# Conv chunks behind blocks 0, 1, 2, 3, and another order of three engines' queues in the last step of layer 0, in a two-layer feed-forward kernel

## The chip, the cores and the metric

One core of one Trainium2 chip (trn2). The metric is the device time of one execution in microseconds (us). The kernel before took 2215.2 us (median of 3 runs, 2212.43 to 2218.39).

## The reference

What is computed, on x of shape (128, 64, 1024), read as 8192 rows of 1024:

```
x = x + L0_ffn(L0_cond(x))     # L0_cond: per batch a 64x64 mixing matrix, made from 8 by a small network with softmax
x = x + L1_ffn(L1_cond(x))     # L1_cond: conv over 9 taps along the 1024, 4 groups of 16 channels, plus a bias per batch
# L0_ffn: x W_base^T + b, plus 8 experts of rank 16, weighed by softmax(gates) minus a threshold, clipped at 0, normalized
# L1_ffn: x W_base^T + b, plus 8 experts of rank 16, weighed by the softmax of the two largest gates
```

## The kernel before, in words

**Tiles and steps.** A tile is 128 rows (two batches) by 1024. There are 64 tiles in layer 0 and 64 in layer 1 and so 128 steps n = 0 to 127; STEPS is 64. `run` (L183) calls each engine's `step(j, par, lay0, lay, lay1, lay2)` with n = 2j + par and the layers of tiles n-1, n, n+1 and n+2; the first two and the last two steps of each layer are written out, the others are a hardware loop. Layer 0 stores its result twice, as rows and as blocks that layer 1 reads. Every product of two fp32 values is made from a high part (fp32r) and a low one (the difference): Xhi/Xlo, Yhi/Ylo, Whi/Wlo, HThi/HTlo.

**A step on TensorE (L911).** For each of KT = 8 blocks k it runs `base` (L847: 9 matmuls of tile n, Yhi and Ylo by Whi and Wlo, into psB), and between blocks it puts three other things: `turn` (L869) of tile n-1, a transpose of the weighed low-rank product hw; `up` (L877) of tile n-1, six matmuls by Bhi/Blo that read HThi and HTlo; and `mix` (L817) of tile n+1 in four chunks c = 0 to 3, in layer 0 the mixing matrix, in layer 1 the conv (six matmuls each, L842 to L844). In the loop over k the order is base, turn, chunks, up. Where they stand is set by hand (L54 to L57):

```
MIX_AFTER = (0, 1, 2, 3)
CONV_AFTER = (0, 0, 1, 1)
TURN_AFTER, UP_AFTER = (4, 2), (5, 3)
```

that is, in layer 1 `turn` stands after k=2 and `up` after k=3. CONV_AFTER holds for chunks of a tile of layer 1, so from step 63 on. Chunks use two halves of psT in turn, so in layer 1 chunk c waits for the side copy of chunk c-2 (side_out, L830). Block 0 waits for half 0 of Yhi and Ylo and for `emit` of tile n-2 (o_done, L854), block 4 for half 1; in step 64 each block also waits for its new weights (w_hi, w_lo, w_loP, L855).

**The other engines in a step of layer 1.** Each works its queue in program order.

- VectorE (L757): `weigh` of tile n-1 (copy ag and the gates, L742 to L734, then hw, L748); `evacuate_y` of tile n+1 (L604) chunk by chunk out of psT; `low_ht` (HTlo, L755), `add_rest` (L633), `add_shifted` of half 0 (L612), `emit` of tile n-1 (three additions, L648), `split_y` of half 0 (Ylo, L618), then half 1 of both.
- ScalarE (L497): its part of the gates, `copy_side` (L460) of the four chunks, the part of the conv's result that belongs to a neighbour; `high_ht` (HThi, L552), `high_x` of tile n+2 (Xhi, L431), `split_y` (Yhi, L447) of each half once `add_shifted` has run.
- GpSimd (L390): `low_x` of tile n+2 (Xlo, L356), `residual` of tile n+1 (L385).
- SyncE (L255): loads Xraw and row of tile n+2, sends the side parts to their neighbours (`shift`, L303, four transfers, after all four copies), stores tile n-1, loads res of tile n+1.

**The last step of layer 0 (n = 63).** Here the weights of layer 1 replace those of layer 0, block by block as `base` is done with them: ScalarE writes Whi (`split_w`, L462, which waits for base_tile > k), VectorE Wlo of even k (L622) and GpSimd Wlo of odd k (`split_lo`, L344). VectorE's order is evacuate_y 0 and 1, split_w 0, evacuate_y 2 and 3, split_w 2, add_shifted and split_y of half 0, low_ht, add_rest, half 1, split_w 4, emit; split_w 6 comes at step 64. ScalarE has copy_side 0 and 1, split_w 0, copy_side 2 and 3, split_w 1 to 3, Yhi of half 0, high_ht, Yhi of half 1, split_w 4 and 5, high_x, split_w 6 and 7. GpSimd has split_lo 1, 3, 5, low_x, split_lo 7, residual.

Of the kernel before, what the change touches and what calls it, by code (L numbers as in the profile page):

```python
# [30 lines left out]
KT = H // P  # L31
# [6 lines left out]
BR = 8  # L38
# [13 lines left out]
STORE0 = 16 * (1 + BG)  # L52
MODES = 8
MIX_AFTER = (0, 1, 2, 3)  # L54
CONV_AFTER = (0, 0, 1, 1)
MIX_AFTER_FIRST = (1, 3, 4, 5)
TURN_AFTER, UP_AFTER = (4, 2), (5, 3)  # L57
PIECES = 4
# [12 lines left out]
def build(nc, x, condw, condr, mixw, l0w, l0b, l0B, convw, l1w, l1b, l1B, out):  # L71
# [8 lines left out]
    with ExitStack() as ctx:  # L80
# [121 lines left out]
        def before(j, par):  # L202

            return (j, 0) if par else (j - 1, 1)

        def after(j, par):

            return (j + 1, 0) if par else (j, 1)
# [123 lines left out]
        def _(pool):  # L332
# [11 lines left out]
            def split_lo(k, layer):  # L344
                pool.wait_ge(w_hi, KT * layer + k + 1)
                w = H + NAG[layer]
                pool.tensor_tensor(Wlo[:, k, 0:w], stage[:, k, 0:w], as_f32(Whi[:, k, 0:w]), ALU.subtract)\
                    .then_inc(w_loP, 1)
# [41 lines left out]
            def step(j, par, lay0, lay, lay1, lay2):  # L390
                n = 2 * j + par
                if isinstance(j, int) and n == 0:

                    pool.wait_ge(w_hi, KT)
                    pool.wait_ge(w_lo, KT // 2)
                    pool.wait_ge(w_loP, KT // 2)
                    pool.memset(craw, 0.0).then_inc(conv_zero, 1)
                if isinstance(j, int) and n == STEPS - 1:
                    for k in range(1, KT - 2, 2):
                        split_lo(k, 1)  # L400
                if lay2 is not None:
                    low_x(j + 1, par, lay2)
                if isinstance(j, int) and n == STEPS - 1:
                    split_lo(KT - 1, 1)
                if lay1 is not None:
                    residual(*after(j, par), lay1)
                if isinstance(j, int) and n == 1:
                    pool.wait_ge(s_hi, 2)
                    pool.tensor_tensor(Blo[:, 1, :], b1raw, as_f32(Bhi[:, 1, :]), ALU.subtract).then_inc(s_loP, 1)
                    pool.wait_ge(s_hi, 3)  # L410
                    pool.tensor_tensor(CT[:, :, 1, :, :], craw, as_f32(CT[:, :, 0, :, :]), ALU.subtract)\
                        .then_inc(s_loP, 1)
# [5 lines left out]
        def _(act):  # L418
# [14 lines left out]
            def high_m(n):  # L433
                act.wait_ge(agg_ready, n + 1)
                nc.scalar.copy(M[0:C, 0, 0:C], agg[0:C, :])
                nc.scalar.copy(M[C:P, 0, C:P], agg[C:P, :]).then_inc(m_hi, 1)
# [10 lines left out]
                    nc.scalar.copy(Yhi[:, par, h * HB:(h + 1) * HB], Y[:, h * HB:(h + 1) * HB])\  # L447
                        .then_inc(yhi_half, 1)

            def copy_side(j, par, c):  # L450

                m = 2 * j + par - STEPS
                act.wait_ge(y_chunk, NC * (m + STEPS) + c + 1)
                if isinstance(m, int) and m == 0:
                    act.wait_ge(agg_ready, STEPS)
                else:
                    act.wait_ge(y_sum, 2 * m)
                bank = psT[:, c % 2, :].rearrange("p (b s t o) -> p b s t o", b=2, s=2, t=BR)
                to = side.rearrange("p h (t b o) -> p b (h t) o", t=REACH, b=BG)
                nc.scalar.copy(to[:, 2 * c:2 * c + 2], bank[:, :, 1]).then_inc(side_out, 1)  # L460

            def split_w(k, layer):  # L462
                act.wait_ge(w_in[k], 16 * (layer + 1))
                if layer:

                    if k < KT - 1:
                        act.wait_ge(base_tile, k + 1)
                    else:
                        act.wait_ge(base_done, STEPS)
                w = H + NAG[layer]  # L470
                nc.scalar.copy(Whi[:, k, 0:w], stage[:, k, 0:w]).then_inc(w_hi, 1)
# [25 lines left out]
            def step(j, par, lay0, lay, lay1, lay2):  # L497
                n = 2 * j + par
                last_of_0 = isinstance(j, int) and n == STEPS - 1
                if lay0 is not None:  # L500
                    weigh(*before(j, par), lay0)
                if lay1 == 1:
                    for c in range(NC):
                        copy_side(*after(j, par), c)
                        if last_of_0 and c == 1:
                            split_w(0, 1)
                if last_of_0:
                    for k in range(1, KT // 2):
                        split_w(k, 1)
                if lay1 == 1 and not last_of_0:  # L510
                    high_ht(*before(j, par))
                    if lay2 is not None:
                        high_x(j + 1, par, lay2)
                if lay1 is not None:
                    split_y(*after(j, par), lay1, range(0, 1))
                if lay1 == 0 and lay2 is not None:
                    high_x(j + 1, par, lay2)
                if (lay1 != 1 or last_of_0) and lay0 is not None:
                    high_ht(*before(j, par))
                if lay1 is not None:  # L520
                    split_y(*after(j, par), lay1, range(1, 2))
                if lay2 == 0:
                    high_m(n + 2)
                if last_of_0:
                    for k in range(KT // 2, KT - 2):
                        split_w(k, 1)
                    high_x(j + 1, par, lay2)
                if isinstance(j, int) and n == 1:
                    act.wait_ge(l1s_in, 16)
                    nc.scalar.copy(Bhi[:, 1, :], b1raw).then_inc(s_hi, 1)  # L530
                    act.wait_ge(conv_in, 16 * 2 * BR)
                    nc.scalar.copy(CT[:, :, 0, :, :], craw).then_inc(s_hi, 1)
                if isinstance(j, int) and n == STEPS - 1:
                    for k in range(KT - 2, KT):
                        split_w(k, 1)

            def weigh(j, par, layer):

# [21 lines left out]
        def _(dve):  # L560
# [196 lines left out]
            def step(j, par, lay0, lay, lay1, lay2):  # L757
                n = 2 * j + par
                last_of_0 = isinstance(j, int) and n == STEPS - 1
                if lay0 is not None:  # L760
                    weigh(*before(j, par), lay0)
                if isinstance(j, int) and n == STEPS:
                    split_w(KT - 2, 1)
                if lay1 == 0:
                    evacuate_y(*after(j, par), 0, range(0, 2))
                    if lay2 == 0:
                        mixing_matrix(n + 2)
                    evacuate_y(*after(j, par), 0, range(2, 3))
                    split_y(*after(j, par), 0, range(0, 1))
                    evacuate_y(*after(j, par), 0, range(3, NC))  # L770
                    if lay0 is not None:
                        low_ht(*before(j, par))
                        add_rest(*before(j, par))
                    split_y(*after(j, par), 0, range(1, 2))
                    if lay2 == 0:
                        low_m(n + 2)
                    if lay0 is not None:
                        emit(*before(j, par), lay0)
                elif last_of_0:
                    evacuate_y(*after(j, par), 1, range(0, 2))  # L780
                    split_w(0, 1)
                    evacuate_y(*after(j, par), 1, range(2, NC))
                    split_w(2, 1)
                    add_shifted(*after(j, par), 0)
                    split_y(*after(j, par), 1, range(0, 1))
                    low_ht(*before(j, par))
                    add_rest(*before(j, par))
                    add_shifted(*after(j, par), 1)
                    split_y(*after(j, par), 1, range(1, 2))
                    split_w(4, 1)  # L790
                    emit(*before(j, par), lay0)
                elif lay1 == 1:
                    evacuate_y(*after(j, par), 1, range(NC))
                    low_ht(*before(j, par))
                    add_rest(*before(j, par))
                    add_shifted(*after(j, par), 0)
                    emit(*before(j, par), lay0)
                    split_y(*after(j, par), 1, range(0, 1))
                    add_shifted(*after(j, par), 1)
                    split_y(*after(j, par), 1, range(1, 2))  # L800
                else:
                    low_ht(*before(j, par))
                    add_rest(*before(j, par))
                    emit(*before(j, par), lay0)
# [172 lines left out]
```

## Time and profile before

| what | value |
|---|---|
| median of 3 runs | 2215.2 us (2212.43 to 2218.39) |
| profiled execution | 2212.12 us, span 2209.8 us |
| mean granted TensorE clock | 0.996 |
| TensorE busy | 2152.9 us (97%), 12684 matmuls |
| VectorE, ScalarE, GpSimd busy | 65%, 23%, 39% |
| chain that ended last | TensorE 92%, VectorE 4%, issue 1%, DMA 1%, ScalarE 1%, GpSimd 1% |

The span runs from the first to the last instruction of the profiled execution. L862 is line 862 of the kernel; `out<-in` names what an instruction writes and reads. A number in square brackets behind a row of a timeline is the time for which that engine stood idle before it, and what ended that. Of matmuls the ends are modelled: several overlap, so their busy times add up to more than the spacing of their starts.

### The profile page before, as it was taken

The numbers are of one execution on the slowest core, as the hardware profiler recorded it, in microseconds if no ns is written. First come the engines' busy times: TensorE is split into PE (matmuls) and PEld (weight loads), VectorE is DVE, ScalarE is ACT, GpSimd is POOL, SyncE is SP. The second block draws the span as 40 slices with busy tenths as digits, with TensorE's granted clock in tenths as the row PEclk, the third lists the DMA queues.
The fourth block names the chain that finished last, engine by engine and source line by source line (L and its number), as shares of the span: only waits on it lengthen the run. The fifth ranks groups of instructions, "written<-read, shape, count | busy, mean of one in ns | idle before, by whom it ended". The sixth has DMA issues, their size and how long they took to land.

```text
span 2209.8 us, 41168 instructions
## 1 busy us (share of the span) xinstructions
PE 2152.9 (97%) x12684; PEld 2097.4 (95%) x12684; DVE 1446.7 (65%) x3539; ACT 503.2 (23%) x1179; POOL 862.6 (39%) x1052
## 2 busy tenths in 40 slices
PE   4999999999999999999899999999999999999998
PEld 4999999999999999999799999999999999999997
DVE  6777777777777777777555655656556665556665
ACT  3212221221222122221322222222222222222221
POOL 5534444343444434344533333333333333333331
PEclk9999999999999999999999999999999999999999
DMA  5433433334343333434444333343333343333432
GB/s 169 129 108 89 112 96 106 102 99 109 89 109 98 105 103 99 109 89 110 149 135 138 119 118 126 117 134 131 117 122 122 128 136 118 120 124 125 132 124 76
DMA packets 163554, 256.34 MB, mean 116 GB/s; under 512 B 21072, under 2 KB 103376, under 8 KB 163536
## 3 DMA queue, kind: packets, MB, share of 16 engines
q1 hardware_dynamic: 163232, 255.55, 37.7%
q10 hardware_dynamic: 304, 0.56, 0.1%
q8 instruction: 9, 0.15, 0.0%
q14 instruction: 9, 0.07, 0.0%
HBM read 122.01 MB, written 100.73 MB: 101 GB/s over the span
## 4 chain that ended last, share of the span: by engine, by line
PE 92%; DVE 4%; issue 1%; DMA 1%; ACT 1%; POOL 1%; DVEq 0%; SPq 0%; ACTq 0%
PE psB L862 71%; PE psB L888 8%; PE psT L838 3%; PE psT L842 3%; PE psT L843 2%; PE psT L844 2%; PE psT L839 1%; PE psB L875 1%; DVE small L729 1%; DVE small L734 0%; DVE small L731 0%; DVE Y L604 0%; DMA shifted<-mixbuf 0%; DMA stage<-in_l0w 0%; ACT mixbuf L460 0%
## 5 line engine op out<-in xcount | busy, mean ns | idle before, releaser
L862 PE MATMUL psB<-Whi,Yhi 128*128 128x384 f32 (+2 forms) x3072 | 736.7, 348 | 5.5 <-issue 5.5
L356 POOL TENSOR_TENSOR Xlo<-Xraw,Xhi 128x256 fp32r<-128x256 f32 x512 | 423.9, 860 | 786.1 <-ACT Xhi L431 786.0
L862 PE MATMUL psB<-Wlo,Yhi 128*128 128x384 f32 (+2 forms) x3072 | 714.1, 340 | 0.0
L862 PE MATMUL psB<-Whi,Ylo 128*128 128x384 f32 (+2 forms) x3072 | 711.7, 340 | 0.0
L862 PEld LDWEIGHTS psB<-Whi,Ylo 128*128 128x128 f32 x3072 | 560.3, 189 | 0.0
L862 PEld LDWEIGHTS psB<-Wlo,Yhi 128*128 128x128 f32 x3072 | 559.7, 189 | 0.0
L862 PEld LDWEIGHTS psB<-Whi,Yhi 128*128 128x128 f32 x3072 | 526.3, 190 | 22.3 <-issue 5.7
L385 POOL TENSOR_TENSOR res<-res,bias 128x256 f32<-128x256 f32 x256 | 183.8, 749 | 394.2 <-DMA res<-x_scratch 394.2
L447 ACT CAST Yhi<-Y 128x512 fp32r<-128x512 f32 x256 | 159.2, 622 | 562.0 <-DVE Y L612 302.6
L375 POOL TENSOR_TENSOR res<-Xraw,bias 128x256 f32<-128x256 f32 x256 | 223.1, 906 | 114.8 <-DVE outb L648 114.8
L648 DVE TENSOR_TENSOR outb<-psB,res 128x384 f32<-128x384 f32 (+1 forms) x384 | 227.8, 683 | 29.1 <-PE psB L888 21.4
L618 DVE TENSOR_TENSOR Ylo<-Y,Yhi 128x512 fp32r<-128x512 f32 x256 | 212.1, 829 | 49.2 <-ACT Yhi L447 49.2
L742 DVE COPY ag<-psB 128x138 f32<-128x138 f32 (+1 forms) x128 | 38.5, 301 | 209.9 <-PE psB L862 209.9
L431 ACT CAST Xhi<-Xraw 128x1024 fp32r<-128x1024 f32 x128 | 134.7, 1052 | 167.2 <-PE psT L839 154.7
L604 DVE TENSOR_TENSOR Y<-psT,row 128x256 f32<-128x256 f32 x256 | 101.9, 417 | 101.0 <-PE psT L844 100.8
L460 ACT COPY mixbuf<-psT 128x256 f32<-128x256 f32 x256 | 89.4, 374 | 316.7 <-DVE Y L604 316.7
L842 PE MATMUL psT<-CT,Xhi 128*128 128x256 f32 x512 | 149.9, 293 | 7.9 <-ACT mixbuf L460 7.2
L838 PE MATMUL psT<-M,Xhi 128*128 128x256 f32 x512 | 132.9, 312 | 22.3 <-DVE M L575 13.2
L755 DVE TENSOR_TENSOR HTlo<-psB,HThi 128x128 fp32r<-128x128 f32 x128 | 37.3, 292 | 174.4 <-ACT HThi L552 174.4
L612 DVE TENSOR_TENSOR Y<-shifted,Y 128x512 f32<-128x512 f32 x128 | 102.8, 803 | 71.7 <-DMA shifted<-mixbuf 71.7
L844 PE MATMUL psT<-CT,Xlo 128*128 128x256 f32 x512 | 145.2, 284 | 0.0
L843 PE MATMUL psT<-CT,Xhi 128*128 128x256 f32 x512 | 145.2, 284 | 0.0
(90 smaller groups left out, 2056.5 us busy)
## 6 DMA issues: line engine op xcount, KB each, us to landing
Xraw<-in_x SPq DMA_DIRECT2D x64, 512.0 KB, 3.4
x_scratch<-outb SPq DMA_DIRECT2D x64, 512.0 KB, 2.7
x_block_scratch<-outb SPq DMA_DIRECT2D x512, 64.0 KB, 2.0
Xraw<-x_block_scratch SPq DMA_DIRECT2D x64, 512.0 KB, 4.9
res<-x_scratch SPq DMA_DIRECT2D x64, 512.0 KB, 4.4
out<-outb SPq DMA_DIRECT2D x64, 512.0 KB, 3.0
shifted<-mixbuf SPq DMA_DIRECT2D x128, 224.0 KB, 2.5
row<-row_scratch SPq DMA_DIRECT2D x128, 64.0 KB, 4.3
```

The source lines that it names most:

```text
L356: last = pool.tensor_tensor(Xlo[:, piece], Xraw[:, par, piece], as_f32(Xhi[:, piece]), ALU.subtract)
L375: last = pool.tensor_tensor(res[:, par, :].rearrange("p (r q) -> p r q", r=BR)[:, r, :], Xraw[:, par, 0:H].rearrange("p (q r) -> p r q", r ...
L385: last = pool.tensor_tensor(res[:, par, piece], res[:, par, piece], bias[:, piece], ALU.add)
L447: nc.scalar.copy(Yhi[:, par, h * HB:(h + 1) * HB], Y[:, h * HB:(h + 1) * HB])\
L618: nc.vector.tensor_tensor(Ylo[:, par, h * HB:(h + 1) * HB], Y[:, h * HB:(h + 1) * HB], as_f32(Yhi[:, par, h * HB:(h + 1) * HB]), ALU.subtr ...
L648: last = nc.vector.tensor_tensor(to[:, r0:r1, :], product, res[:, par, :].rearrange("p (r q) -> p r q", r=BR)[:, r0:r1, :], ALU.add)
L838: mm(to, Xhi[:, xs], M[:, :, :].rearrange("p s n -> p (s n)"), start=True, stop=False)
L842: mm(to, Xhi[:, xs], hi, start=True, stop=False)
L843: mm(to, Xhi[:, xs], lo, start=False, stop=False)
L844: last = mm(to, Xlo[:, xs], hi, start=False, stop=True)
L862: last = mm(psB[:, 3 * par + b, 0:cols], y, w[:, k, BANK0[b]:BANK0[b] + cols], start=(k == 0 and y is yh and w is Whi), stop=(k == KT - 1 ...
L888: last = mm(psB[:, 3 * par + b, :], y[:, :], w[:, layer, b * HB:(b + 1) * HB], start=False, stop=(y is HTlo), skip_group_check=True)
```

## The change

CONV_AFTER becomes (0, 1, 2, 3). In the last step of layer 0 the order of the queues is another: VectorE takes evacuate_y of all chunks, split_w 0 and 2, low_ht, add_rest, half 0 of Y, emit, half 1; its split_w 4 and 6 move to step 64, behind chunks 1 and 3. ScalarE interleaves split_w with the rest and has high_ht and high_x ahead of the halves of Y. GpSimd has split_lo 1 and 3, low_x, split_lo 5 and 7. `copy_side` takes a range of chunks and waits for y_sum or agg_ready at chunk 0 only. The other steps keep their order.

```diff
-CONV_AFTER = (0, 0, 1, 1)
+CONV_AFTER = (0, 1, 2, 3)
...
                 if isinstance(j, int) and n == STEPS - 1:
-                    for k in range(1, KT - 2, 2):
+                    for k in range(1, KT // 2, 2):
                         split_lo(k, 1)
                 if lay2 is not None:
                     low_x(j + 1, par, lay2)
                 if isinstance(j, int) and n == STEPS - 1:
-                    split_lo(KT - 1, 1)
+                    for k in range(KT // 2 + 1, KT, 2):
+                        split_lo(k, 1)
...
-            def copy_side(j, par, c):
+            def copy_side(j, par, chunks):
...
+                for c in chunks:
+                    act.wait_ge(y_chunk, NC * (m + STEPS) + c + 1)
+                    if c == 0:
+                        if isinstance(m, int) and m == 0:
+                            act.wait_ge(agg_ready, STEPS)
+                        else:
+                            act.wait_ge(y_sum, 2 * m)
...
+                elif last_of_0:
+                    split_w(0, 1)
+                    split_w(1, 1)
+                    copy_side(*after(j, par), range(0, 2))
+                    split_w(2, 1)
+                    copy_side(*after(j, par), range(2, NC))
+                    split_w(3, 1)
+                    high_ht(*before(j, par))
+                    high_x(j + 1, par, lay2)
+                    split_w(4, 1)
+                    split_y(*after(j, par), 1, range(0, 1))
+                    split_w(5, 1)
+                    split_w(6, 1)
+                    split_y(*after(j, par), 1, range(1, 2))
+                    split_w(7, 1)
+                elif lay1 == 1:
+                    copy_side(*after(j, par), range(NC))
                     high_ht(*before(j, par))
                     if lay2 is not None:
                         high_x(j + 1, par, lay2)
...
+                    split_y(*after(j, par), 1, range(2))
...
-                if isinstance(j, int) and n == STEPS:
-                    split_w(KT - 2, 1)
...
                 elif last_of_0:
-                    evacuate_y(*after(j, par), 1, range(0, 2))
+                    evacuate_y(*after(j, par), 1, range(NC))
                     split_w(0, 1)
-                    evacuate_y(*after(j, par), 1, range(2, NC))
                     split_w(2, 1)
+                    low_ht(*before(j, par))
+                    add_rest(*before(j, par))
                     add_shifted(*after(j, par), 0)
                     split_y(*after(j, par), 1, range(0, 1))
-                    low_ht(*before(j, par))
-                    add_rest(*before(j, par))
+                    emit(*before(j, par), lay0)
                     add_shifted(*after(j, par), 1)
                     split_y(*after(j, par), 1, range(1, 2))
-                    split_w(4, 1)
-                    emit(*before(j, par), lay0)
                 elif lay1 == 1:
-                    evacuate_y(*after(j, par), 1, range(NC))
+                    evacuate_y(*after(j, par), 1, range(0, 2))
+                    if isinstance(j, int) and n == STEPS:
+                        split_w(4, 1)
+                    evacuate_y(*after(j, par), 1, range(2, NC))
+                    if isinstance(j, int) and n == STEPS:
+                        split_w(6, 1)
                     low_ht(*before(j, par))
                     add_rest(*before(j, par))
                     add_shifted(*after(j, par), 0)
```

## Rows read from the trace of the kernel before

**Rows 1.** TensorE's waits over the whole span: engine line <- what it waited for: us in total, times, longest.

```profile
...
PE psB L888 <- DVE HTlo L755: 7.7, 2, 6.9
PE psT L842 <- ACT mixbuf L460: 7.2, 16, 2.6
...
```

**Rows 2.** The transposes (line 875) of layer 1: count, ns min/median/max, first and last start.

```profile
...
L875 PE MATMUL psB<-ident,hw x63: 270/270/270, 1099.9 to 2175.6; 128*128 128x128 f32 x63
...
```

**Rows 3.** TensorE's timeline, two transposes of layer 1: start, us, engine, line, operation.

```profile
...
1465.02 0.27 PE L875 MATMUL psB<-ident,hw 128*128 128x128 f32 x1
...
1482.16 0.27 PE L875 MATMUL psB<-ident,hw 128*128 128x128 f32 x1
...
```

**Rows 4.** TensorE's timeline, first matmuls of steps 63, 64 and 65.

```profile
...
1060.48 0.70 PE L862 MATMUL psB<-Whi,Yhi 128*128 128x384 f32 x3
...
1087.07 0.34 PE L862 MATMUL psB<-Whi,Yhi 128*128 128x384 f32 x1
...
1109.36 0.34 PE L862 MATMUL psB<-Whi,Yhi 128*128 128x384 f32 x1
...
```

**Rows 5.** TensorE's timeline, one step of layer 1: blocks 0 and 2, first chunk, `up`.

```profile
...
1612.65 0.70 PE L862 MATMUL psB<-Whi,Yhi 128*128 128x384 f32 x3
...
1614.25 0.28 PE L842 MATMUL psT<-CT,Xhi 128*128 128x256 f32 x1
...
1618.79 0.70 PE L862 MATMUL psB<-Whi,Yhi 128*128 128x384 f32 x3
...
1622.10 0.40 PE L888 MATMUL psB<-Bhi,HThi 128*128 128x512 f32 x1
...
```

**Rows 6.** The same step on VectorE and ScalarE, in brackets the idle time before and its cause.

```profile
...
1616.30 0.74 DVE L604 TENSOR_TENSOR Y<-psT,row 128x256 f32<-128x256 f32 x2
...
1616.82 0.65 ACT L460 COPY mixbuf<-psT 128x256 f32<-128x256 f32 x2 [3.15 <-DVE Y L604]
...
1618.99 0.42 DVE L604 TENSOR_TENSOR Y<-psT,row 128x256 f32<-128x256 f32 x1 [0.29 <-PE psT L844]
...
1619.45 0.37 ACT L460 COPY mixbuf<-psT 128x256 f32<-128x256 f32 x1 [0.35 <-DVE Y L604]
...
1620.68 0.27 ACT L552 CAST HThi<-psB 128x128 fp32r<-128x128 f32 x1 [0.86 <-PE psB L875]
...
1620.98 0.29 DVE L755 TENSOR_TENSOR HTlo<-psB,HThi 128x128 fp32r<-128x128 f32 x1 [1.57 <-ACT HThi L552]
...
1622.68 0.69 DVE L612 TENSOR_TENSOR Y<-shifted,Y 128x512 f32<-128x512 f32 x1 [1.07 <-DMA shifted<-mixbuf]
...
1627.84 0.69 DVE L618 TENSOR_TENSOR Ylo<-Y,Yhi 128x512 fp32r<-128x512 f32 x1 [0.69 <-ACT Yhi L447]
...
```

**Rows 7.** The timeline at the kernel's end: HTlo, then the last `up`.

```profile
...
2202.57 0.29 DVE L755 TENSOR_TENSOR HTlo<-psB,HThi 128x128 fp32r<-128x128 f32 x1 [0.72 <-ACT HThi L552]
...
2203.01 0.70 PE L888 MATMUL psB<-Bhi,HThi 128*128 128x512 f32 x2 [0.77 <-DVE HTlo L755]
...
2203.55 0.63 PE L888 MATMUL psB<-Blo,HThi 128*128 128x512 f32 x2
...
```

**Rows 8.** VectorE's weight subtractions (line 625): ns min/median/max, first and last start.

```profile
...
L625 DVE TENSOR_TENSOR Wlo<-stage,Whi x8: 1357/1370/3089, 21.3 to 1093.1; 128x1162 fp32r<-128x1162 f32 x4, 128x1160 fp32r<-128x1160 f32 x4
...
```

**Rows 9.** VectorE's timeline in the last step of layer 0: shifted part added, tile 62 emitted.

```profile
...
1077.63 0.69 DVE L612 TENSOR_TENSOR Y<-shifted,Y 128x512 f32<-128x512 f32 x1 [4.25 <-DMA shifted<-mixbuf]
...
1083.92 1.34 DVE L648 TENSOR_TENSOR outb<-psB,res 128x384 f32<-128x384 f32 x3
...
```

**Rows 10.** TensorE after two waits (timeline), then both stretches with clock (PEclk), by engine.

```profile
...
80.82 0.38 PE L838 MATMUL psT<-M,Xhi 128*128 128x256 f32 x1 [2.21 <-DVE Y L599]
...
1095.26 0.45 PE L842 MATMUL psT<-CT,Xhi 128*128 128x256 f32 x1 [2.56 <-ACT mixbuf L460]
...
81.00:85.00 4.00, 4.00 (x18) 4.00 (x19) 3.54 (x7) 0.62 (x1) 0.00 (x0) 0.58 1.02 414
1095.26:1098.83 3.57, 3.57 (x15) 3.57 (x16) 0.85 (x2) 0.92 (x3) 1.86 (x3) 0.52 0.00 0
...
```

More of the change, by code:

```diff
@@ L448, in split_y @@
                         .then_inc(yhi_half, 1)
-            def copy_side(j, par, c):
+            def copy_side(j, par, chunks):
                 m = 2 * j + par - STEPS
[L453 to L460, printed above, removed]
+                for c in chunks:
[5 more added lines that the diff above has]
+                            act.wait_ge(y_sum, 2 * m)
+                    bank = psT[:, c % 2, :].rearrange("p (b s t o) -> p b s t o", b=2, s=2, t=BR)
+                    to = side.rearrange("p h (t b o) -> p b (h t) o", t=REACH, b=BG)
+                    nc.scalar.copy(to[:, 2 * c:2 * c + 2], bank[:, :, 1]).then_inc(side_out, 1)
             def split_w(k, layer):
@@ L501, in step @@
                     weigh(*before(j, par), lay0)
[L502 to L510, printed above, removed]
+                if lay1 == 0:
+                    split_y(*after(j, par), 0, range(0, 1))
+                    if lay2 is not None:
+                        high_x(j + 1, par, lay2)
+                    if lay0 is not None:
+                        high_ht(*before(j, par))
+                    split_y(*after(j, par), 0, range(1, 2))
+                    if lay2 == 0:
+                        high_m(n + 2)
+                elif last_of_0:
[5 more added lines that the diff above has]
+                    split_w(3, 1)
+                    high_ht(*before(j, par))
+                    high_x(j + 1, par, lay2)
+                    split_w(4, 1)
[6 more added lines that the diff above has]
+                    copy_side(*after(j, par), range(NC))
                     high_ht(*before(j, par))
@@ L513, in step @@
                         high_x(j + 1, par, lay2)
[L514 to L518, printed above, removed]
-                    high_ht(*before(j, par))
[L520 to L527, printed above, removed]
+                    split_y(*after(j, par), 1, range(2))
+                else:
+                    high_ht(*before(j, par))
                 if isinstance(j, int) and n == 1:
@@ L532, in step @@
                     nc.scalar.copy(CT[:, :, 0, :, :], craw).then_inc(s_hi, 1)
-                if isinstance(j, int) and n == STEPS - 1:
-                    for k in range(KT - 2, KT):
-                        split_w(k, 1)
             def weigh(j, par, layer):
```

## The prediction

> **What bounds the kernel now.** I read the page first: TensorE's busy share stands in the table of the profile above and leaves 3% of the span, so the other engines matter only where TensorE waits for them. The table of who waited for whom comes next [rows 1]: layer 1 holds 7.2 us of waits of conv matmuls (L842) for ScalarE's copies of a chunk's side parts, and one wait of 6.9 us in the last step of layer 0, where `up` (L888) needs HTlo. That table leaves out the tails of matmuls, so I measured the steps themselves by TensorE's transposes (`turn`, L875), one in a step. Between the first and the last of layer 1's 63 of them lie 1075.7 us [rows 2], 62 steps, 17.35 us each; a step in which nothing is waited for takes 17.14 [rows 3]. So all that layer 1's steps can gain is 1075.7 - 62 x 17.14 = 13.0 us, and around the change of layers there is a second, larger loss: steps 63 and 64 start at 1060.48 and 1087.07 and step 65 at 1109.36 [rows 4], 48.88 us for what takes 34.28 undisturbed, a loss of 14.6. Nothing else that the change touches can give time back: 27.6 us, 1.2%, is its ceiling.
>
> **Where a step of layer 1 has its slack.** In the timeline of one step [rows 5] a base block takes 1.60 us (1612.65 to 1614.25), chunks 0 and 1 follow at 0.72 each (the 6.14 us to 1618.79 less two blocks, over four, less a few hundredths of waiting), then block 1, chunks 2 and 3, block 2, the transpose, block 3 and `up` at 1622.10. The last chunk ends at 1618.79; `up` comes 3.31 us later. In that gap VectorE takes chunk 3 out of PSUM (1618.99), ScalarE copies its side part (1619.45), makes HThi (1620.68), and VectorE makes HTlo (1620.98) [rows 6]. The programs fix this order: ScalarE has high_ht behind all four copy_side, VectorE has low_ht behind all four evacuate_y. It costs nothing today, because two base blocks and a transpose lie between chunk 3 and `up`.
>
> **Part 1, CONV_AFTER (0, 1, 2, 3), the term that decides.** Chunk 3 moves behind block k=3. UP_AFTER[1] stays 3, and in a pass over k TensorE issues the chunk before `up`. So `up`, which waits for ht_hi and ht_lo, now follows chunk 3 with nothing between. What must pass in that hole, counted from the moment when TensorE could have started `up`: to evacuate_y of chunk 3, 0.20 us (1618.79 to 1618.99); to its side copy, 0.46 (to 1619.45); to HThi, right behind the copy on ScalarE, 0.28 (a copy is busy 0.37, and the second of two copies back to back starts 0.28 after the first: the pair takes 0.65 [rows 6]); to HTlo, 0.30 (1620.68 to 1620.98); from HTlo to `up`, 0.44, from the end of the kernel, where nothing else lies between (2202.57 to 2203.01). Sum 1.68. Restarting costs 0.07 more: there the first pair of `up`'s matmuls is busy 0.70, the next 0.63 [rows 7]. So **1.75 us a step**. Bounds: 1.5, if the last matmul's tail covers 0.2 of it; 2.1, if HTlo (busy 0.29) is stretched as VectorE's weight subtraction was beside GpSimd, from 1.37 to 3.09 [rows 8], which adds 0.36. It happens wherever conv and `up` of k=3 share a step, steps 64 to 126: 63 x 1.75 = **+110.3 us**. Nothing hides it: TensorE's queue is in order and is what sets the end.
>
> What the same edit takes away: chunk 2 may start once chunk 0's side copy is done. The gates (L742 to L748) hold VectorE until 3.65 us into the step (1616.30), so that copy ends at about 3.65 + 0.46 + 0.37 = 4.5, and chunk 2 is due at 2 x 1.60 + 2 x 0.72 = 4.6: any delay of the gates shows. The new place is 3 x 1.60 + 2 x 0.72 = 6.2 in, late enough even with the gates 0.7 behind. All 13.0 us go: **-13.0**.
>
> What else moves with chunk 3, by 3.3 us: SyncE's four shift transfers, and behind them in its queue the store, the res load and the next Xraw load. Chunk 3 leaves PSUM at about 9.5 into the step; the first add_shifted starts 3.23 after the side copy (1619.45 to 1622.68), that is at 13.2; then emit and both Ylo, as long as now (5.85, from 1622.68 to 1628.53), to 19.0. The step is then 18.9 long, so VectorE is just done when base_done comes, and the gates have 1.6 us to spare before the transpose and chunk 2. Ylo of half 0 is ready two microseconds early, o_done too. Xhi starts at 10.5 and Xlo ends near 15, before 20.5 where it is due; the Xraw load, issued near 17.6, has over 10 us. I take 0 for all of this; it costs something only if that tail grows by over 1.6 us.
>
> ScalarE's copy_side in one call saves three waits already met: 0.
>
> **Part 2, the last step of layer 0.** Today TensorE sits 6.9 us at `up` because ScalarE and VectorE keep HThi and HTlo behind half 0 of Y, which waits for a shift transfer until 1077.63 [rows 9]. Now they come first, and that wait falls to 0.4 to 2 us (two weight splits of 1.37 stand ahead of HTlo [rows 8]). What is late next: emit of tile 62 now stands behind the first Ylo, and block 0 of step 64 waits for o_done of that tile. The transfer is still late, since the weight, Xraw and bias loads ahead of it don't change. From 1077.63: 2.1 us to the end of the first Ylo (add 0.7, cast 0.6, subtract 0.7, handovers), 1.34 for emit [rows 9], so step 64 starts at about 1081.3, against 1087.07: -5.8. In step 64 the weighing starts late, behind half 1 of Y and ScalarE's last split, which I put at 1.7, and split_w(6) stands ahead of HTlo, 1.37; 17.14 + 1.7 + 1.37 = 20.2 against 22.29: -2.1 (its share of the 63 stalls is counted above). GpSimd's splits of k=5 and 7 move behind Xlo of tile 65; they are due ten microseconds later in step 64, 0. Together **-8**, between 0 (a new wait replaces each one removed) and -14.6.
>
> **Sum.** 110.3 - 13.0 - 8 = +89.3 us. The profiled execution took 2212.1 us (span 2209.8, and 2.3 around it that the change doesn't touch), so 2301.4; the median shown, 2215.2, is 3.1 above it: **2304.5**. By the bounds of the stall, 63 x 1.5 and 63 x 2.1, and of part 2: 2215.2 + 94.5 - 13 - 14.6 = 2282, and 2215.2 + 132.3 - 13 = 2334.
>
> **Rivals.**
> A, the clock. TensorE's granted clock fell after a wait of 2.56 us: 0.52 over the next 3.57 us, about the lower of its two levels (1.2 against 2.4 GHz), a loss of 3.57 x 0.48 = 1.7 us; it also fell after one of 2.21 (0.58 in the four microseconds from 81) [rows 10]. If the new wait did this in each step, 63 x 1.7 = 107 more: 2412. For it: the wait comes every step. Against: the profile will show it as about 1.5 us (the matmul's tail taken off), shorter than any wait after which the clock fell here, and today's waits of up to 0.4 leave it alone. Chance 0.05.
> The Trainium skill, "TensorE: Matmul & The Clock Gate", section "A second HAM failure mode: psum-queue depth-cycling", says that frequent short idles between groups of matmuls can make the clock swing between half and full rate. By that rule rival A would be the outcome; this trace, which idles briefly in many steps of layer 1 and has a mean clock of 0.996 all the same, doesn't bear it out for the shortest ones.
> B, VectorE becomes the second bound. If GpSimd's Xlo now overlaps emit and add_shifted worse than today, or the shift transfers land 3 us later, the tail passes the 1.6 us of slack and the gates hold chunk 2 and the transpose. 1 us beyond it costs 63: 2368. Against: the order of these operations and their spacing are the same as now. Chance 0.04.
> C, faster. The edit does what it is for, and `up` isn't held: the change is then -13 - 8 = -21, or 2194. The place is the handover from chunk 3 to HTlo; it decides at 21 / 63 = 0.33 us, below which the kernel gains. The chain as read is 1.68, and HTlo can't overtake chunk 3 on VectorE. Chance 0.03, with 0.01 for a result within 0.3%, which is about what a measurement of this kernel can tell from no change.
> Forecast: 0.88. Hence slower 0.96, same 0.01, faster 0.03, and a range of 2282 to 2334, which the forecast's own bounds fill.
>
> **What would show it.** Right: in the table of waits, TensorE L888 waiting for HTlo some 63 times, 1.5 us each, about 95 us in total; L842's wait for ScalarE's copy gone from layer 1; transposes 18.9 us apart, first to last in layer 1 about 1172; layer 0's steps at their old length; no 6.9 us wait, but a wait of L862 near 1080 for emit (L648). Wrong: transposes still 17.1 to 17.4 apart (rival C), a granted clock well under 1.0 in the middle of layer 1 (A), or TensorE waiting in `turn` or at chunk 2 (B).

## The result

The changed kernel takes 2299.5 us (median of 5 runs, 2297.2 to 2301.4) against 2215.2 for the kernel before (by now of 5 as well, 2211.5 to 2218.4): 1.038 times as long (95% interval 1.037 to 1.040). That is 84.3 us slower by the medians and 87.9 by the two profiled spans, which the page of the profile after shows with the busy shares and the chain that ended last:

```profile
span 2297.7 us, 40976 instructions
...
PE 2160.0 (94%) x12684; PEld 2104.6 (92%) x12684; DVE 1374.6 (60%) x3539; ACT 502.2 (22%) x1179; POOL 855.0 (37%) x1052
...
PE 92%; DVE 3%; issue 1%; ACT 1%; DMA 1%; POOL 0%; ACTq 0%; SPq 0%; DVEq 0%
```

TensorE does the same 12684 matmuls and is busy for 94% where it was 97%. Who it waited for (total us, times, longest), and its transposes in layer 1 (count, ns min/median/max, first and last start):

```profile
PE psB L895 <- DVE HTlo L761: 96.3, 64, 2.1
...
PE psB L869 <- issue: 7.9, 2, 5.2
...
PE psT L849 <- ACT mixbuf L463: 0.2, 1, 0.2
```

```profile
L882 PE MATMUL psB<-ident,hw x63: 270/270/270, 1086.7 to 2259.0; 128*128 128x128 f32 x63
```

The first row answers to [rows 1]: `up` (now L895) waits for HTlo 64 times, 96.3 us, where it was 7.7 in two; the conv's wait for the side copy has gone from 7.2 us to 0.2. From the first to the last transpose it is 1172.3 us, 1075.7 in [rows 2]. The hole in one step, the counterpart of [rows 5] and [rows 6]:

```profile
1619.98 0.28 PE L849 MATMUL psT<-CT,Xhi 128*128 128x256 f32 x1
...
1620.57 0.28 PE L851 MATMUL psT<-CT,Xlo 128*128 128x256 f32 x1
1620.89 0.42 DVE L610 TENSOR_TENSOR Y<-psT,row 128x256 f32<-128x256 f32 x1 [1.89 <-PE psT L851]
1621.35 0.37 ACT L463 COPY mixbuf<-psT 128x256 f32<-128x256 f32 x1 [1.95 <-DVE Y L610]
1621.61 0.27 ACT L558 CAST HThi<-psB 128x128 fp32r<-128x128 f32 x1
...
1621.92 0.29 DVE L761 TENSOR_TENSOR HTlo<-psB,HThi 128x128 fp32r<-128x128 f32 x1 [0.61 <-ACT HThi L558]
...
1622.36 0.70 PE L895 MATMUL psB<-Bhi,HThi 128*128 128x512 f32 x2 [1.51 <-DVE HTlo L761]
...
1622.90 0.63 PE L895 MATMUL psB<-Blo,HThi 128*128 128x512 f32 x2
...
1624.56 1.02 DVE L618 TENSOR_TENSOR Y<-shifted,Y 128x512 f32<-128x512 f32 x1 [2.02 <-DMA shifted<-mixbuf]
```

The last six matmuls are chunk 3's, 0.12 apart, so `up` could have started at 1620.69. Behind them come the evacuation (1620.89), the side copy (1621.35), HThi (1621.61), HTlo (1621.92) and `up` (1622.36): 0.20, 0.46, 0.26, 0.31 and 0.44, in all 1.67. In brackets stands 1.51, since the profile takes off the last matmul's tail.

Then the change of layers (before: [rows 4], [rows 9]):

```profile
1074.86 0.74 DVE L618 TENSOR_TENSOR Y<-shifted,Y 128x512 f32<-128x512 f32 x1 [3.22 <-DMA shifted<-mixbuf]
...
1076.34 1.09 DVE L624 TENSOR_TENSOR Ylo<-Y,Yhi 128x512 fp32r<-128x512 f32 x1 [0.74 <-ACT Yhi L448]
1077.36 1.34 DVE L654 TENSOR_TENSOR outb<-psB,res 128x384 f32<-128x384 f32 x3
...
1078.91 0.41 PE L869 MATMUL psB<-Whi,Yhi 128*128 128x384 f32 x1 [2.63 <-issue]
...
1090.83 1.37 DVE L631 TENSOR_TENSOR Wlo<-stage,Whi 128x1160 fp32r<-128x1160 f32 x1
...
1092.12 0.28 DVE L761 TENSOR_TENSOR HTlo<-psB,HThi 128x128 fp32r<-128x128 f32 x1
...
1092.55 0.70 PE L895 MATMUL psB<-Bhi,HThi 128*128 128x512 f32 x2 [2.09 <-DVE HTlo L761]
```

Step 63 starts at 1058.68 and step 64 at 1078.91, 20.23 us where it was 26.59: the first Ylo, emit (1077.36 to 1078.70), then block 0. Its row says `issue`, no releaser that the profile found; that it was emit is read from the 0.21 us between them, and from the run below that moves emit. Step 65 starts at 1101.94, 23.03 later, where it was 22.29: split_w(6) (it stood in step 64 before too, right behind the gates, and now stands behind chunk 3) starts at 1090.83 and pushes HTlo to 1092.12, and `up` waits 2.09 us instead of 1.51. The granted clock (PEclk, the first number behind the five engines) fell after both long waits and stayed up through layer 1:

```profile
1078.90:1083.00 4.10, 4.09 (x17) 4.10 (x18) 2.77 (x5) 2.24 (x5) 1.76 (x2) 0.61 0.66 193
1092.50:1096.50 4.00, 3.96 (x13) 3.55 (x14) 2.54 (x6) 0.62 (x1) 3.26 (x4) 0.62 0.42 130
1117.00:2259.00 1142.00, 1051.61 (x6242) 1022.41 (x6241) 560.73 (x1520) 244.38 (x544) 368.62 (x484) 1.00 0.35 114
```

**Where the 87.9 us of span come from**: steps 65 to 126 start to start (1101.94 to 2271.66, before 1109.36 to 2185.12), +94.0; steps 63 and 64, -5.6; layer 0 up to step 63 -1.8 and the last step with the end +1.4. The latter two are not the change's: in the ten runs below, whose layer 0 is the same up to there, step 63 starts anywhere between 1058.0 and 1060.0, a spread as wide as this difference, and at the end the clock fell around the same 2.33 us wait that it survived before.

### The profile page after: what moved, and what is told of

It is laid out like the page before. It is cut to its first block, busy times and chain, and to the rows that moved or that the text cites. A ratio compares the mean times of both kernels' runs of the same rounds, so it can differ in the third digit from the quotient of the medians.

```text
span 2297.7 us, 40976 instructions
## 1 busy us (share of the span) xinstructions
PE 2160.0 (94%) x12684; PEld 2104.6 (92%) x12684; DVE 1374.6 (60%) x3539; ACT 502.2 (22%) x1179; POOL 855.0 (37%) x1052
## 4 chain that ended last, share of the span: by engine, by line
PE 92%; DVE 3%; issue 1%; ACT 1%; DMA 1%; POOL 0%; ACTq 0%; SPq 0%; DVEq 0%
PE psB L869 70%; PE psB L895 8%; PE psT L845 3%; PE psT L851 3%; PE psT L849 3%; PE psT L850 3%; PE psT L846 1%; DVE Y L610 1%; DVE HTlo L761 1%; ACT HThi L558 1%; PE psB L882 1%; DMA stage<-in_l0w 0%; POOL Wlo L347 0%; DMA shifted<-mixbuf 0%; DMA outb<-in_condw 0%
## 5 line engine op out<-in xcount | busy, mean ns | idle before, releaser
L610 DVE TENSOR_TENSOR Y<-psT,row 128x256 f32<-128x256 f32 x256 | 108.6, 425 | 366.7 <-PE psT L851 364.2
L463 ACT COPY mixbuf<-psT 128x256 f32<-128x256 f32 x256 | 95.1, 372 | 498.3 <-DVE Y L610 498.3
L895 PE MATMUL psB<-Bhi,HThi 128*128 128x512 f32 x256 | 85.6, 416 | 96.3 <-DVE HTlo L761 96.3
L895 PEld LDWEIGHTS psB<-Bhi,HThi 128*128 128x128 f32 x256 | 42.8, 189 | 108.0 <-ACT HThi L558 105.4
```

The costliest lines, as they stand in the source:

```text
L895: last = mm(psB[:, 3 * par + b, :], y[:, :], w[:, layer, b * HB:(b + 1) * HB], start=False, stop=(y is HTlo), skip_group_check=True)
```

## The experiments

Theory 1 is the prediction's: the handover from chunk 3 through ScalarE and VectorE to `up`, 1.75 us in each of 63 steps. Ratios are to the kernel before on the same chip (2208 to 2210 us in those runs); the changed kernel itself was not run again beside them, so where 2299.5 is set against them, it is across chips. "Step" below is the mean distance of the transposes of steps 65 to 126: 17.35 before, 18.87 after.

**The two halves of the change, apart.** The first:

```diff
-CONV_AFTER = (0, 0, 1, 1)
+CONV_AFTER = (0, 1, 2, 3)
```

> Before, with CONV_AFTER (0, 1, 2, 3) alone; the last step of layer 0 keeps its queues. Theory 1 (the handover from chunk 3 to HTlo stands in front of up in each of 63 steps, 1.75 us each; the queue order has no part in it): 2215 + 110 - 13 for the old waits at chunk 2 - 3 to 4 for the 2.56 us wait in step 64 = about 2308, with 63 waits of up for HTlo of 1.5 us and the 6.9 us wait still there. Rival (the new queue order of ScalarE and VectorE holds TensorE, and up's wait only shows it): within 20 us of 2215.

Measured: 2303.8 us, ratio 1.043 (1.041 to 1.045), step 18.87; 95.4 us above the kernel before on that chip (2208.4), where 93 was expected. TensorE's waits of `up`:

```profile
PE psB L888 <- DVE HTlo L755: 103.1, 65, 7.4
```

This is the whole loss, with the old queue order: 63 waits of 1.5 (steps 64 to 126), the long wait of step 63, 7.4, and the last `up`'s, 0.8. The second half, the change with that line put back:

```diff
-CONV_AFTER = (0, 1, 2, 3)
+CONV_AFTER = (0, 0, 1, 1)
```

> After, with CONV_AFTER back at (0, 0, 1, 1). Theory 1: no wait at up in layer 1; the queue order alone gives 4 to 10 us at the change of layers, so about 2207, with the small waits at chunk 2 (13 us in sum) back. Rival (queue order is the cost): near 2299.

Measured: 2203.5 us, ratio 0.9975 (0.9966 to 0.9985), step 17.30. The waits at chunk 2 are back (1.6 us in step 63, where chunk 0's side copy now stands behind two weight splits, and 3.4 in step 64, where the gates are late), `up`'s wait is left at the end alone:

```profile
PE psT L849 <- ACT mixbuf L463: 8.4, 12, 3.4
...
PE psB L895 <- DVE HTlo L761: 0.8, 1, 0.8
```

So the queue order is a small gain, 5 us, and has no part in the loss.

**Undoing the handover alone.** Chunks stay behind k = 0, 1, 2, 3:

```diff
-                    copy_side(*after(j, par), range(NC))
+                    copy_side(*after(j, par), range(0, 3))
                     high_ht(*before(j, par))
+                    copy_side(*after(j, par), range(3, NC))
...
-                    evacuate_y(*after(j, par), 1, range(2, NC))
+                    evacuate_y(*after(j, par), 1, range(2, 3))
+                    low_ht(*before(j, par))
+                    evacuate_y(*after(j, par), 1, range(3, NC))
                     if isinstance(j, int) and n == STEPS:
                         split_w(6, 1)
-                    low_ht(*before(j, par))
```

> After, but in the steps of layer 1 high_ht stands ahead of the fourth copy_side on ScalarE and low_ht ahead of the fourth evacuate_y on VectorE; chunks stay behind k=0, 1, 2, 3. Theory 1: HTlo is ready about a microsecond before up is due, the 63 waits vanish, 2299.5 - 63 x 1.75 = 2189, layer 1's transposes 17.14 apart. Rival 2 (it is the four separate places of the chunks, or the shift transfers, emit and Y coming 3.3 us later, that hold TensorE): over 2250, with the wait moved to block 0, o_done or chunk 2.

Measured: 2188.3 us, ratio 0.9908 (0.9892 to 0.9925); repeated, 2188.5 and 0.9905 (below). Step 17.13, from 17.12 to 17.14 in all 61. Its timeline:

```profile
1602.98 0.37 ACT L463 COPY mixbuf<-psT 128x256 f32<-128x256 f32 x1 [2.04 <-DVE Y L611]
...
1603.25 0.27 ACT L559 CAST HThi<-psB 128x128 fp32r<-128x128 f32 x1
...
1603.55 0.29 DVE L762 TENSOR_TENSOR HTlo<-psB,HThi 128x128 fp32r<-128x128 f32 x1 [0.61 <-ACT HThi L559]
...
1604.64 0.63 PE L897 MATMUL psB<-Bhi,HThi 128*128 128x512 f32 x2
...
1605.30 0.38 ACT L463 COPY mixbuf<-psT 128x256 f32<-128x256 f32 x1 [1.78 <-DVE Y L611]
```

HTlo (1603.55) now stands ahead of chunk 3's copy (1605.30), and `up` starts at 1604.64 without a wait. Everything else that came later with chunk 3 is still late (the shift transfers, emit, Y), so none of it held TensorE: rival 2 of that run falls.

**Is the hole a sum of its links?** ScalarE's half of that edit alone:

```diff
-                    copy_side(*after(j, par), range(NC))
+                    copy_side(*after(j, par), range(0, 3))
                     high_ht(*before(j, par))
+                    copy_side(*after(j, par), range(3, NC))
```

> After, with ScalarE's half of the former alone: high_ht ahead of the fourth copy_side, VectorE's order as it is. Theory 1, the chain is a sum of links: copy and HThi (0.46 + 0.28 + 0.30) leave it, VectorE's own 0.33 from chunk 3 to HTlo takes their place, so 0.20 + 0.33 + 0.44 + 0.07 = 1.04 us a step instead of 1.75: 2299.5 - 63 x 0.71 = 2255, waits of up of about 0.8 us each. Rival 3 (only the last handover to up counts, or the wait comes from VectorE alone): no gain, 2299, or the whole of it, 2189.

Measured: 2256.0 us, ratio 1.0215 (1.0198 to 1.0232), step 18.16, that is 1.03 above the step without a wait; 1.04 was expected.

```profile
1601.13 0.27 ACT L559 CAST HThi<-psB 128x128 fp32r<-128x128 f32 x1
...
1602.72 0.42 DVE L611 TENSOR_TENSOR Y<-psT,row 128x256 f32<-128x256 f32 x1 [1.89 <-PE psT L852]
1603.06 0.28 DVE L762 TENSOR_TENSOR HTlo<-psB,HThi 128x128 fp32r<-128x128 f32 x1
1603.18 0.37 ACT L463 COPY mixbuf<-psT 128x256 f32<-128x256 f32 x1 [1.78 <-DVE Y L611]
...
1603.49 0.70 PE L896 MATMUL psB<-Bhi,HThi 128*128 128x512 f32 x2 [0.81 <-DVE HTlo L762]
```

HThi (1601.13) is done long before; VectorE goes from chunk 3 (1602.72) to HTlo (1603.06) in 0.34, and `up` follows 0.43 later. One link more, in the other direction, was ScalarE's Xhi ahead of HThi:

```diff
                     copy_side(*after(j, par), range(NC))
-                    high_ht(*before(j, par))
                     if lay2 is not None:
                         high_x(j + 1, par, lay2)
+                    high_ht(*before(j, par))
```

> After, with ScalarE's high_x (1.06 us) ahead of high_ht in layer 1: the chain gets a link of about 0.97 us, the wait of up grows from 1.51 to about 2.5 us a step. Theory 1, every link counts at its full length: 62 x 0.97 = 60 more, 2360, if the clock stays. Rival A of the prediction, the clock falls after waits of this size: each fall about 1.7 us more, so up to 2465 if it falls in every step, and the granted clock of layer 1 well below 1.0. The trace has one fall after a wait of 2.1 and one after 2.6 and none after the 1.5 of 62 steps; I expect falls in a part of the steps, 2380 to 2440.

Measured: 2398.5 us, ratio 1.086 (1.085 to 1.088). `up` waits 2.45 us in each step, and the clock falls in every second one:

```profile
1499.76 0.27 PE L882 MATMUL psB<-ident,hw 128*128 128x128 f32 x1
...
1505.51 0.70 PE L895 MATMUL psB<-Bhi,HThi 128*128 128x512 f32 x2 [2.45 <-DVE HTlo L761]
1506.05 0.63 PE L895 MATMUL psB<-Blo,HThi 128*128 128x512 f32 x2
...
1519.56 0.27 PE L882 MATMUL psB<-ident,hw 128*128 128x128 f32 x1
...
1525.33 1.20 PE L895 MATMUL psB<-Bhi,HThi 128*128 128x512 f32 x2 [2.45 <-DVE HTlo L761]
1526.32 1.05 PE L895 MATMUL psB<-Blo,HThi 128*128 128x512 f32 x2
...
1540.72 0.27 PE L882 MATMUL psB<-ident,hw 128*128 128x128 f32 x1
```

From transpose to transpose it is 19.80 us, then 21.16, and so on to the end, 31 long and 30 short of 61. In a short one the pairs of `up` are 0.54 and 0.47 apart, in a long one 0.99 and 0.85. The granted clock behind the two waits (first number behind the five engines):

```profile
1505.51:1509.51 4.00, 4.00 (x21) 3.73 (x22) 2.92 (x5) 0.62 (x1) 2.71 (x4) 1.00 0.33 108
1525.33:1529.33 4.00, 4.00 (x13) 3.42 (x14) 1.93 (x4) 0.62 (x1) 2.67 (x4) 0.63 0.34 107
```

The short step is 0.94 above 18.86, the link that was put in; the long one pays 1.36 more for the clock. 61 x 0.94 + 31 x 1.36 = 99.5, and 2398.5 - 99.5 = 2299.0, within a microsecond of the changed kernel's time.

**Covering the handover instead of shortening it.** Two ways of putting one block of 1.60 us between chunk 3 and `up`:

```diff
-TURN_AFTER, UP_AFTER = (4, 2), (5, 3)
+TURN_AFTER, UP_AFTER = (4, 2), (5, 4)
```

> After, with up of layer 1 behind block k=4 instead of k=3: the queues as they are, only the consumer moves. Theory 1: the handover of 1.68 us from the end of chunk 3 now has a block of 1.60 to hide under, so about 0.1 us a step stays: 2299.5 - 63 x 1.65 = 2196, a little above the run with HThi and HTlo ahead of chunk 3. Rival 2 (late emit and Y become the bound once up moves another 1.6 us back): VectorE's tail passes the end of the step, TensorE waits at block 0 or for the gates, 2215 or more.

Measured: 2201.0 us, ratio 0.9958 (0.9942 to 0.9975), step 17.31. And, in a kernel of its own:

```diff
-CONV_AFTER = (0, 1, 2, 3)
+CONV_AFTER = (0, 1, 2, 2)
```

> After, with CONV_AFTER (0, 1, 2, 2): chunk 3 follows chunk 2 at once and up keeps its place behind k=3. Theory 1: again one block of 1.60 us covers a chain of 1.68, about 0.1 us a step stays, 2299.5 - 63 x 1.65 = 2196; chunk 2's small waits don't come back, since chunk 2 keeps its place. Rival (any conv chunk moved late costs in proportion): half of the loss, near 2250.

Measured: 2198.5 us, ratio 0.9949 (0.9932 to 0.9965), step 17.26. Both give the loss back but for 0.18 and 0.13 us a step over 17.13: the cover is 0.08 short of the chain, and the restart is paid. In one step with `up` behind k=4:

```profile
1628.54 0.69 PE L869 MATMUL psB<-Whi,Yhi 128*128 128x384 f32 x3
...
1629.78 0.29 DVE L761 TENSOR_TENSOR HTlo<-psB,HThi 128x128 fp32r<-128x128 f32 x1 [0.61 <-ACT HThi L558]
...
1630.21 0.70 PE L895 MATMUL psB<-Bhi,HThi 128*128 128x512 f32 x2
...
1631.68 0.70 PE L869 MATMUL psB<-Whi,Yhi 128*128 128x384 f32 x3
```

`up` follows HTlo by 0.43, the link of the chain. The block ahead of it takes 1.67 us and `up` 1.47, against 1.60 and 1.40 in the kernel without a wait: 0.14 of the 0.18. Both landed 2 to 5 us above the expectation, which had taken 0.1: 61 x 0.18 = 11 and 61 x 0.13 = 8 are most of the 12.5 and 10 us above the 2188.5 of the kernel without a wait. No wait row of the profile shows these, because the matmul's tail hides them; only the steps' length does.

**The change of layers.** First split_w(6) of step 64, put behind low_ht in the changed kernel:

```diff
                     evacuate_y(*after(j, par), 1, range(2, NC))
+                    low_ht(*before(j, par))
                     if isinstance(j, int) and n == STEPS:
                         split_w(6, 1)
-                    low_ht(*before(j, par))
```

> After, with split_w(6) of step 64 behind low_ht instead of ahead of it. In after that step's up waited 2.1 us and the clock fell. Theory: the split added 0.6 us to that one wait and the fall of the clock 1.5; moved, the wait is 1.5 like the others, the clock stays, and the stretch from step 63's transpose on to step 65's is 2.1 us shorter; 2297, hardly to be told from 2299.5 by time, so the trace has to say. Rival: a wait of 1.5 makes the clock fall there too.

Measured: 2298.2 us, ratio 1.041 (1.039 to 1.043), not to be told from the changed kernel by time. In the trace step 64's wait is like all others, and the distance of its transpose to the next is 19.24 us instead of 21.41, 2.17 less for 0.58 less of waiting; the granted clock is 1.00 in the 4 us behind the wait, where it was 0.62:

```profile
1091.80 0.70 PE L895 MATMUL psB<-Bhi,HThi 128*128 128x512 f32 x2 [1.51 <-DVE HTlo L761]
```

Then the kernel with HThi and HTlo first, with and without emit of tile 62 ahead of half 0 of Y:

```diff
                     add_rest(*before(j, par))
+                    emit(*before(j, par), lay0)
                     add_shifted(*after(j, par), 0)
                     split_y(*after(j, par), 1, range(0, 1))
-                    emit(*before(j, par), lay0)
```

> The kernel with HThi and HTlo ahead of chunk 3 once more, beside the next one on the same chip: 2188, a ratio to before of 0.991.

> The same, and in the last step of layer 0 VectorE has emit of tile 62 ahead of half 0 of Y. Theory: block 0 of step 64 waited 2.6 us for that emit behind the first Ylo; with emit in the gap before the shift transfer lands, the block waits for Ylo only, which is 1.3 us earlier, and the clock may not fall: 1.3 to 3 us less than its neighbour, step 64 starting near 1077.5. Rival (the transfers and splits around it set the start): no difference in step 64's start.

Measured: 2188.5 and 2188.1 us (0.9905 and 0.9903, intervals of 0.0016 either way), no difference by time. By the traces step 63 is shorter, 19.16 against 20.23 us:

```profile
1073.43 1.35 DVE L655 TENSOR_TENSOR outb<-psB,res 128x384 f32<-128x384 f32 x3 [1.49 <-PE psB L897]
...
1075.46 1.15 DVE L619 TENSOR_TENSOR Y<-shifted,Y 128x512 f32<-128x512 f32 x1 [0.67 <-DMA shifted<-mixbuf]
...
PE psB L884 <- DVE hw L755: 3.3, 2, 2.3
...
PE psB L871 <- ACT Yhi L448: 1.6, 1, 1.6
```

emit runs in the gap before the shifted part lands, and block 0 waits 1.6 us for Yhi instead of 2.6 for emit. The clock stays up behind that shorter wait (1.00 over the next 4 us, 0.57 in the run beside it). Steps 63 and 64 together take 38.26 us against 39.36, so 1.1 us is saved, below the 1.3 to 3 expected: `turn` of step 64 now waits 1.0 us for hw (3.3 in two waits, 2.3 in one without this edit) and the chunk behind it 0.4, which is what is late next.

## Why the prediction was right

**The handover.** 1.68 by rows, 1.67 in the trace after; with the restart 1.75 predicted, and the steps say 18.87 - 17.13 = 1.74. The five links came from three places of the kernel before, the last one from its end [rows 7], and none was off by more than 0.02. The shortened and the lengthened chain changed the step by what the links say.

**The gain in the steps.** -13.0 was taken as all of the excess over 17.14. Chunk 2's waits are gone, and the kernel without the handover runs at 17.13 in each step; from step 65's start to the last step's it takes 1061.85 us where the kernel before took 1075.76, 13.9 less.

**The change of layers.** -8 was predicted, and without step 64's share of the stall it is -5.6 - 1.74 = -7.4. That the sum came so near is in part luck, for its parts missed in both directions. Step 63 I had at 20.8 us and it took 20.2: the shifted part landed 16.2 us into the step and not 17.2, though its transfers were issued 2.5 us later in it (at 1068.99, 10.3 in, against 1068.33, 7.9 in). With the queues alone changed they were issued 11.5 in and landed at 16.3, so it isn't the issue that sets the landing; what took a microsecond off isn't known. The 0.4 to 2 us foreseen at `up` of step 63 did not come at all. Step 64 I had at 20.2 and the stall of 1.75, 21.95, and it was 23.03. The 1.7 for late gates didn't come (the wait at chunk 2 was 0.15 us), and the split ahead of HTlo lengthened `up`'s wait by 0.6 and not by 1.37. What came in their place are the clock's two falls, which I had not counted: behind the wait of 2.6 for emit, and behind that of 2.1. By their windows above they lost 4.10 x 0.39 + 4.00 x 0.38 = 3.1 us.

**The rest of the sum.** 110.3 - 13.0 - 8 = +89.3 against 87.9 in span and 84.3 in medians; the range held it. Of the 5.0 us between 2304.5 and 2299.5, 3.1 came in with the median before, which lies that much above its profiled run; after, the two are the same run.

**The rivals.** A, the clock: it stayed up after every one of the 62 waits of 1.51 us. But the prediction was close to its edge: with one microsecond more the clock fell in every second step. B: TensorE waited neither for the gates nor for Y; VectorE was even less loaded (see below). C: no step came without its wait.

## What to carry to other kernels

When work is spread out to relieve one wait, list for each piece that moves what its helpers do after it in their queues, and which later instruction needs that: here the wait was for HTlo, which has no data from the chunk at all and only stands behind it in two queues. A price for such a wait can be summed from start-to-start distances of the old trace, link by link; the cure is to move the small operation ahead in both queues, which made the same placement 0.9% faster than the kernel before instead of 3.8% slower. A block of cover that is a tenth of a microsecond too short leaves a loss that no wait row shows.

## What the runs showed of the hardware

**The clock after waits.** It fell behind single waits of 2.1 and 2.6 us in one kernel, and behind every second one of 2.45 us in another, but behind none of the 62 waits of 1.51 us. The wait of 2.33 us at the end was followed by a full clock in the kernel before and by half in the changed one (1.00 and 0.50 over the next 4 us). And a wait of 3.45 us, 46 us into the kernel, was followed by 1.00 in the kernel before and by 0.57 in the run with CONV_AFTER alone. So between 2.1 and 3.5 us length alone doesn't decide. A fall cost 1.4 to 1.6 us on top of the wait. The Trainium skill, "TensorE: Matmul & The Clock Gate", section "A second HAM failure mode: psum-queue depth-cycling", says that short idles which come often make the clock swing; here that held at 2.45 us and not at 1.51.

**VectorE's gates beside GpSimd.** In the changed kernel GpSimd's residual starts after the gates (1613.90 against their end at 1613.86). It isn't the longer step that does it: the load of res stands behind the shift transfers in SyncE's queue and comes 2.9 us later in the step, 17.05 us in where it was 14.16 (medians of 50 steps), and the run with HThi and HTlo first, whose step is 17.13, has the short gates too (226 to 228 ns). One operation of the gates, before and after (ns min/median/max):

```profile
L731 DVE SCALAR_TENSOR_TENSOR small<-iota,small x62: 225/646/793, 1111.0 to 2169.6; 128x8 f32<-128x8 f32 x62
```

```profile
L737 DVE SCALAR_TENSOR_TENSOR small<-iota,small x56: 227/227/227, 1122.4 to 2160.1; 128x8 f32<-128x8 f32 x56
```

A median of 646 ns became 227, and VectorE's busy time fell from 1446.7 to 1374.6 us over the kernel, though it does the same work. The Trainium skill, "SBUF — State Buffer", section "Who interferes with whom", has VectorE and GpSimd share a pair of ports; the trace agrees in direction. Of this operation's 64 in layer 1 of the kernel before, the 58 that overlap a GpSimd instruction have a median of 649 ns, and the six that don't take 225 to 227. That it is the ports, no run here shows.
